# Pairing loads issued in halves, and a new slot table, in a four-block transformer kernel on one core

## The reference

```python
for i in range(DEPTH):
    x = attn_layer(shift_tokens(x), Wqkv[i], q_scale[i], k_scale[i], Wo[i]) + x
    x = ffn_layer(shift_tokens(x), ln_g[i], ln_b[i], W1[i], b1[i], W2[i], b2[i]) + x
# attn_layer: 16 heads of 64, q and k normalised and rotated; windows of 32 tokens
bk2, bv2 = (look(bk), look(bv))          # each window sees itself and the one before
attn = jax.nn.softmax(sim, -1)           # sim masked outside the band
out = jnp.einsum('bhwij,bhwje->bhwie', attn, bv2)
# ffn_layer: layer norm, x @ W1, a * gelu(gate), @ W2
```

## Time and profile before

| | us |
|---|---|
| median of 3 runs (lowest to highest) | 2043.94 (2038.4 to 2044.57) |
| the profiled execution | 2045.6 |
| its span | 2044.3 |
| PE busy, share | 1886.4, 92% |
| ACT, DVE, POOL busy | 1609.5, 1577.7, 1069.5 |
| granted TensorE clock, mean | 0.974 |

### The profile page before, as it was taken

How to read it: one execution, slowest core, us unless ns; L and a number is a source line. 1 busy time by engine, 2 the same in 40 slices (tenths; PEclk the granted TensorE clock), 3 DMA queues, 4 the chain that set the end, 5 groups by cost and what they waited for, 6 DMA issues and landing times.

```text
span 2044.3 us, 78892 instructions
## 1 busy us (share of the span) xinstructions
PE 1886.4 (92%) x34797; PEld 1592.2 (78%) x34797; DVE 1577.7 (77%) x2229; ACT 1609.5 (79%) x2835; POOL 1069.5 (52%) x523
## 2 busy tenths in 40 slices
PE   6999999678999999999999899999999998999986
PEld 4888888657887787877878777788788787887865
DVE  4556664677888798988889787988889788889873
ACT  2577777567898888888888888888788888888864
POOL 3100000366567575667566665758666576656520
PEclk9999999889999999999999999999999999999998
DMA  5000000033233334243332424344333334333421
GB/s 169 11 7 5 5 6 6 1 101 103 80 103 104 108 100 122 82 128 104 99 111 80 127 83 114 94 121 107 103 101 107 102 92 118 90 107 85 114 73 31
DMA packets 119822, 174.01 MB, mean 85 GB/s; under 512 B 25303, under 2 KB 44346, under 8 KB 119482
## 3 DMA queue, kind: packets, MB, share of 16 engines
q1 hardware_dynamic: 119308, 168.92, 29.8%
q10 hardware_dynamic: 174, 0.05, 0.0%
HBM read 117.54 MB, written 51.38 MB: 83 GB/s over the span
## 4 chain that ended last, share of the span: by engine, by line
PE 65%; ACT 13%; issue 8%; POOL 8%; DVE 6%; DMA 0%; POOLq 0%; ACTq 0%; SPq 0%; DVEq 0%
PE bank L705 7%; PE bank L855 6%; PE bank L682 6%; PE bank L684 5%; PE bank L683 5%; PE s_pair L727 5%; PE o_pair L756 4%; POOL rt L1703 3%; PE bank L609 3%; POOL rt L1694 3%; PE bank L768 3%; ACT t L1044 3%; PE bank L877 2%; ACT L1102 2%; PE bank L739 2%
## 5 line engine op out<-in xcount | busy, mean ns | idle before, releaser
L1694 POOL TENSOR_TENSOR rt<-raw,rot 128x1024 f32<-128x1024 f32 x192 | 456.5, 2378 | 343.6 <-PE bank L705 284.7
L1703 POOL TENSOR_TENSOR rt<-rt,t 128x2048 f32<-128x2048 f32 x96 | 439.8, 4582 | 142.5 <-DVE t L1497 138.5
L682 PE MATMUL bank<-wqkv_hi,xs 128*128 128x512 f32 x576 | 250.3, 435 | 24.7 <-ACT vn L1053 12.0
L1036 ACT ACTIVATE raw<-bank 128x512 f32<-128x512 f32 x384 | 230.0, 600 | 35.7 <-PE bank L684 15.1
L705 PE MATMUL bank<-const,rt 128*128 128x128 f32 x1536 | 221.7, 283 | 21.3 <-issue 9.8
L1505 DVE TENSOR_TENSOR rt<-rt,bank 128x2048 f32<-128x2048 f32 x96 | 219.6, 2288 | 18.2 <-POOL rt L1703 15.2
L684 PE MATMUL bank<-wqkv_hi,xs 128*128 128x512 f32 x576 | 230.9, 401 | 0.0
L683 PE MATMUL bank<-wqkv_lo,xs 128*128 128x512 f32 x576 | 230.3, 400 | 0.4 <-issue 0.4
L1497 DVE TENSOR_TENSOR t<-raw,bank 128x1024 f32<-128x1024 f32 x192 | 225.1, 1214 | 0.6
L1518 DVE TENSOR_REDUCE sm<-s_pair 128x16 f32<-128x1024 f32 x96 | 117.6, 1225 | 138.1 <-PE s_pair L727 137.7
L1484 DVE TENSOR_REDUCE bank<-t 128x32 f32<-128x2048 f32 x96 | 219.3, 2284 | 3.7 <-ACT t L1044 3.7
(11 more groups left out here) (413 smaller groups left out, 4489.1 us busy)
## 6 DMA issues: line engine op xcount, KB each, us to landing
v<-v_rows SPq DMA_DIRECT2D x288, 256.0 KB, 4.3
v_rows<-vn SPq DMA_DIRECT2D x192, 256.0 KB, 4.6
v<-v_rows SPq DMA_DIRECT2D x96, 192.0 KB, 3.1
wraw<-in_L_ffn_Wqkv_dram SPq DMA_DIRECT2D x36, 256.0 KB, 2.9
wo<-in_L_ffn_Wo_dram SPq DMA_DIRECT2D x6, 512.0 KB, 4.0
wraw<-in_L_ffn_W_in_dram SPq DMA_DIRECT2D x8, 256.0 KB, 2.7
w_out<-in_L_ffn_W_out_dram SPq DMA_DIRECT2D x8, 256.0 KB, 3.1
wraw<-in_L_ffn_W_dram SPq DMA_DIRECT2D x12, 170.5 KB, 2.3
```

The source lines that it names most:

```text
L682: pe.matmul(bank[:, :], hi, w[0][:, :], start=True, stop=False)
L1036: act.activation(k.raw_r[c][:, n * 512:(n + 1) * 512], k.one.at["qk", j][:, :], ACT.Copy)\
L1694: e = pool.tensor_tensor(heads(k.rt_r[c][:, part]), heads(k.raw_r[c][:, part]), cosv, ALU.mult)
L1703: pool.tensor_tensor(k.rt_r[c][:, :], k.rt_r[c][:, :], k.t2[:, :], ALU.add).then_inc(s["rot_add"], 1)
```

## The change

`pair_values(c)` becomes `pair_values(c, half)`, which issues two of the four loads; the waits stand in the first half. The two halves have slots of their own in `SP_AT`. All numbers of all tables are new. The core of the diff (of the tables, one pair of lines):

```diff
-ATTENTION_START, ATTENTION_SPACING = 7, 40
-EXPERTS_START, EXPERTS_SPACING = 71, 40
-LATE_START, LATE_SPACING = 391, 32
+ATTENTION_START, ATTENTION_SPACING = 6, 40
+EXPERTS_START, EXPERTS_SPACING = 70, 40
+LATE_START, LATE_SPACING = 372, 32
...
-SP_AT = dict(gain=9, w0=13, w1=13, w2=19, w3=19, st00=31, st01=43, st10=43, st11=43, w4=43, pair0=44, w5=63, pair1=73,
-             wo=114, w6=142, w7=148, w2d=181)
+SP_AT = dict(gain=26, w0=54, w1=72, w2=74, w3=76, st00=77, st01=79, st10=80, st11=86, w4=86, pair00=87, pair01=93,
+             w5=99, pair10=109, pair11=138, wo=169, w6=210, w7=210, w2d=221)
...
-        def pair_values(c):
+        def pair_values(c, half):
             v = 2 * u + c
-            sp.wait_ge(s[f"st_v{c}"], 32 * (u + 1))
-            if u:
-                sp.wait_ge(s["pe_o"], v - 1)
-            else:
-                sp.wait_ge(s["zero_kv"], ZEROS)
-            for half in range(2):
-                g0 = 1 if c == 0 and half == 0 else 0
...
+            if half == 0:
+                sp.wait_ge(s[f"st_v{c}"], 32 * (u + 1))
+                if u:
+                    sp.wait_ge(s["pe_o"], v - 1)
+                else:
+                    sp.wait_ge(s["zero_kv"], ZEROS)
+            g0 = 1 if c == 0 and half == 0 else 0
...
-        yield from t.to("pair0")
-        pair_values(0)
+        yield from t.to("pair00")
+        pair_values(0, 0)
+        yield from t.to("pair01")
+        pair_values(0, 1)
         yield from t.to("w5")
         next_chunk(5)
-        yield from t.to("pair1")
-        pair_values(1)
+        yield from t.to("pair10")
+        pair_values(1, 0)
+        yield from t.to("pair11")
+        pair_values(1, 1)
```

More of the change, by code:

```diff
@@ L158, in to @@
             yield
-ATTENTION_START, ATTENTION_SPACING = 7, 40
-EXPERTS_START, EXPERTS_SPACING = 71, 40
-LATE_START, LATE_SPACING = 391, 32
[L165 to L175, removed]
-             ln_sd_d=113, ln_out_d=113)
@@ new lines @@
+EXPERTS_START, EXPERTS_SPACING = 70, 40
+LATE_START, LATE_SPACING = 372, 32
+PE_A = dict(ln_sq_a=8, ln_sd_a=8, ln_out_a=12, features=19, k_features=32, q_features=32, sums=41, kv_turn=45,
+            quotient=45, norm0=52)
+PE_B = dict(ln_sq_b=8, ln_sd_b=8, ln_out_b=17, top2=17, weights=22, combine=27, expert0=34, expert1=36, expert2=44,
+            expert3=47, expert4=49, expert5=60, expert6=60, expert7=63, expert8=68, moe_out=74, ln_sq_c=75,
+            ln_sd_c=75, ln_out_c=79, scores=79, exp=79, threshold=96, spT=103, attend=107, back=114, ln_sq_d=118,
+            ln_sd_d=118, ln_out_d=118)
@@ new lines @@
+ACT_A = dict(ln_sq_a=6, ln_sd_a=6, ln_out_a=14, features=14, k_features=14, q_features=14, sums=40, kv_turn=42,
+             quotient=42, norm0=42)
+ACT_B = dict(ln_sq_b=0, ln_sd_b=0, ln_out_b=13, top2=13, weights=13, combine=25, expert0=29, expert1=32, expert2=36,
+             expert3=37, expert4=42, expert5=50, expert6=58, expert7=58, expert8=58, moe_out=68, ln_sq_c=71,
+             ln_sd_c=71, ln_out_c=74, scores=74, exp=74, threshold=86, spT=86, attend=86, back=106, ln_sq_d=113,
+             ln_sd_d=113, ln_out_d=113)
@@ new lines @@
+DVE_A = dict(ln_sq_a=0, ln_sd_a=13, ln_out_a=19, features=23, k_features=36, q_features=36, sums=36, kv_turn=51,
+             quotient=51, norm0=56)
+DVE_B = dict(ln_sq_b=0, ln_sd_b=14, ln_out_b=20, top2=23, weights=25, combine=34, expert0=36, expert1=42, expert2=50,
+             expert3=50, expert4=55, expert5=63, expert6=65, expert7=68, expert8=70, moe_out=76, ln_sq_c=76,
+             ln_sd_c=79, ln_out_c=80, scores=80, exp=89, threshold=89, spT=106, attend=109, back=115, ln_sq_d=115,
+             ln_sd_d=125, ln_out_d=125)
@@ new lines @@
+POOL_B = dict(ln_sq_b=0, ln_sd_b=0, ln_out_b=0)
+PE_AT = dict(qk00=35, qk01=36, qk02=36, qk03=37, qk10=46, qk11=50, qk12=54, qk13=54, v00=67, v01=68, v10=70, v11=70,
+             tqk00=72, tqk01=74, tqk02=81, tqk03=82, tqk10=83, tqk11=83, s00=83, tqk12=83, tqk13=83, s01=84, s10=93,
+             tp00=103, tp01=103, s11=105, a00=105, a01=113, tp10=120, tp11=124, to00=127, to01=130, a10=131, a11=131,
+             to10=137, to11=138, wo=147, mean=152, var=163, up0=176, up1=177, up2=177, down=188)
@@ new lines @@
+ACT_AT = dict(xs=8, qk00=24, qk01=26, qk02=27, qk03=27, sq0=32, qk10=39, norm0=42, qk11=42, qk12=46, qk13=49, sq1=51,
+              norm1=55, v00=55, v01=57, v10=60, v11=61, tqk00=62, tqk01=71, tqk02=73, tqk03=73, tqk10=77, tqk11=77,
+              tqk12=78, tqk13=78, exp0=87, tp00=94, tp01=94, exp1=106, tp10=115, tp11=118, to00=118, to01=119,
+              to10=127, to11=134, xf=141, lnsq=148, rstd=151, gelu0=168, gelu1=168, gelu2=168)
+DVE_AT = dict(ss0=41, sin0=48, nrm0=63, ss1=64, sin1=66, nrm1=77, smax0=90, ssum0=104, smax1=104, oa0=119, ssum1=119,
+              oa1=132, z_mid=145, xc=155, hn=161, hh0=171, hh1=171, hh2=172, z_out=192)
@@ L201 @@
+POOL_AT = dict(xs=43, zero=51, w0=75, cos0=80, w1=80, add0=92, w2=93, w3=93, cos1=94, add1=94, w4=99, w5=108, w6=192,
+               w7=235)
+SP_AT = dict(gain=26, w0=54, w1=72, w2=74, w3=76, st00=77, st01=79, st10=80, st11=86, w4=86, pair00=87, pair01=93,
+             w5=99, pair10=109, pair11=138, wo=169, w6=210, w7=210, w2d=221)
 SIGNALS = (
@@ L1824, in store_values @@
                 .then_inc(s[f"st_v{c}"], 16)
-        def pair_values(c):
+        def pair_values(c, half):
             v = 2 * u + c
-            sp.wait_ge(s[f"st_v{c}"], 32 * (u + 1))
-            if u:
-                sp.wait_ge(s["pe_o"], v - 1)
-            else:
-                sp.wait_ge(s["zero_kv"], ZEROS)
-            for half in range(2):
-                g0 = 1 if c == 0 and half == 0 else 0
[L1835 to L1839, removed]
+            if half == 0:
[5 more added lines that the diff above has]
+            g0 = 1 if c == 0 and half == 0 else 0
+            first = (NW * c + g0 - 1 + half) * WIN
+            for r in range(2):
+                at = 2 * WIN * r + WIN * half
+                src = k.v_rows[u % 2, first:first + (NW - g0) * WIN, r, :].rearrange("(g j) e -> j g e", j=WIN)
+                sp.dma_start(k.v2_r[c][at:at + WIN, g0:, :], src).then_inc(s[f"v2_{c}"], 16)
         t = Slots(SP_AT)
```

## The result

| | before | after |
|---|---|---|
| median of 4 runs each (lowest to highest), us | 2042.06 (2038.4 to 2044.57) | 2021.33 (2019.5 to 2024.43) |
| the profiled execution and its span, us | 2045.6, 2044.3 | 2024.43, 2023.1 |

After to before is 0.9901, with a 95% interval from 0.988 to 0.9923. The change gains 21 us. The forecast was 49 us (1995). Its sign held, and so did the wide range (1970 to 2030); the forecast's own range ended at 2020, just short, and the size did not hold.

A forecast was written before the change was run, and what follows sets the result against it. PE was taken as the bound, losing idle time to instruction holes behind value transfers and to the lower clock. 38 + 5 + 8 - 2 = 49 us off the profiled 2045.6, forecast 1995; own range 1970 to 2020, 8 in 10 1970 to 2030.

The forecast's parts named there:

- Item 1: SP's list: spreading the value transfers ends PE's instruction holes in attend of chunk 0; 38 us, plus 5 at the drain.
- the 43 with its drain: Gain from SP's new list: 38 us for the holes and 5 for the hole at 1966 us, where the last units drain.
- So it should not starve: Scores of chunk 0 begin after 1082.5, the second burst (1.5 MB) ends by 1080.7, so PE keeps its instructions.
- the clock's 15 us: Work lost over the six layers because the mean granted clock is 0.99; counted beside the 29.7 us of holes.
- Item 3: ACT's list: xs and one kT ahead of raw1, hidden by 0.3 us before PE's second transposes; 2 us lost, ends 0 and 23.
- Item 2: SP's moved half of v21 lands before attend of chunk 1 needs it, slack 8 us; cost 0.
- excess, five times: At layer changes SP's waits for POOL's weight splits may delay v21 loads, costing the lateness five times; taken as 0.
- Item 4: Start of the six layers: threshold work moved behind unit 0's normalisation and sum; gain 8 us, ends 0 and 12.0.
- Item 5: Block 0's tables, where PE's list changes too: a gain or loss up to 12.0 us, taken as 0.
- Rival 1: Holes move to the scores of chunk 0 behind the six-load burst, overlapping output weights' load; half stays, 2016 us; chance 0.13.
- Rival 2: Holes are not from the burst, or crossing an instruction block costs what it costs; 2038 us; chance 0.10.
- Rival 3: ACT's new order becomes the bound, raw1 late ahead of PE's second transposes every unit; slower, 2053 us; chance 0.07.

The follow-up runs named there:

- kernel 2: The changed kernel with SP's old list (v21's four loads together, v20's four together); 1.0025 of the kernel before.
- kernel 3: kernel 1 with POOL's sixth weight split (w5) one step earlier, ahead of the rotation of chunk 0; 0.9881 of the kernel before.
- kernel 4: The changed kernel with stores and pairing loads moving 16 of their 512 columns from unit 2 on; 0.9818 of the kernel before.
- kernel 5: The changed kernel with POOL's xs put back behind the rotation of chunk 0; 0.9838 of the kernel before.
- kernel 11: kernel 5 with the last two v21 loads held until PE ended the next unit's chunk 0 scores; 0.9762 of the kernel before, median 1989.7 us.
- kernel 1: The kernel before with only SP's list of the change, all other tables and the start old; 1.0004 of the kernel before.
- kernel 6: The changed kernel with the last sequence's sparse attention threshold ahead of unit 0's normalisation again; 0.9918 of the kernel before.

## Why the prediction was right in sign and wrong in size

*Item 1, the holes, is the step that failed*, in its sentence "The holes go". The mechanism stands: packets of instructions waited behind the values, and undoing the split brings the long holes back (kernel 2). The size does not. A hole has a part of its own, 1.15 us at this place with next to nothing in the queues, and the smaller burst leaves 1.70. I took the one unit in the earlier trace rows that passed the place as a sign that the place is free of holes unless a packet is late; that a packet must be due there I had written myself, and one that is due costs over a microsecond there with the queues empty too. Issue time fell by 12.3 us where I counted on 34.2 (29.7 and 4.5). Measured by itself item 1 is 22 to 27 us (kernels 2 and 3), against the 43 with its drain. The 43 are near what the transfers of the values cost in all: kernels 2 and 4 are 2.1% apart, 42 us, some 5 of them kernel 2's waits for weights. The split takes 22 to 25 of these and leaves 17 to 20. "So it should not starve", said of the second burst, failed with it: L727 lost 6.2 us, and splitting that burst took 16 us off kernel 5 (kernel 11).

*The terms that were not there.* The prediction priced SP's, ACT's and DVE's new lists and not POOL's, though POOL's is in the diff. Its `xs` ahead of the rotation cost 13 to 16 us in time (kernel 5): 10.7 at L768 and 9.8 of PE's busy time, in the profile. That is why only a part of the clock's 15 us came back: the long holes went and ten waits of 1.65 to 2.2 us came. The forecast had 28 us too much: item 1 accounts for 16 to 21 of them and this term for 13 to 16; item 3's 2 us, which were not lost, go the other way.

*Item 2, the moved half of `v21`, 0.* Right for this kernel, by a list that I had not priced. I named the waits for POOL's splits and the "excess, five times"; kernel 1 shows it at 14.8 us. The change avoids it because POOL's `w5` moved ahead of the rotation (kernel 3). The zero should have had that condition.

*Item 3, ACT's list, -2.* No wait of L705 for `raw` is in the profile. ACT's `raw` ends at 1067.97 us in an ordinary unit, and the block of transposes behind the output matrix begins at 1067.86 (1.04 us); its second half, which needs the bank, begins near 1068.4. So 0.4 us were to spare where the prediction had 0.3, and it cost 0. ACT's old list was not tried by itself.

*Item 4, the start, 8.* 6.2 us by kernel 6's profile, though its time does not settle it, and its cause as told: DVE serves unit 0 first, ACT waits 2.63 us for the square root's sum where it waited 8.03, PE 6.23 where it waited 9.7 (5 or less was forecast):

```profile
398.24 0.23 ACT L1110 ACTIVATE rn<-rn 128x32 f32<-128x32 f32 x1 [2.63 <-DVE rn L1486]
...
399.27 0.80 PE L682 MATMUL bank<-wqkv_hi,xs 128*128 128x512 f32 x1 [6.23 <-ACT vn L1053]
...
400.38 0.16 DVE L1414 RECIPROCAL e_small<-e_small 128x2 f32<-128x2 f32 x1
```

*Item 5, block 0, 0.* Not told from 0: kernel 3 with block 0's old lists has the first output matrix at 476.0 us, kernel 6 with the new ones and the old threshold at 475.2.

*The sum, as the runs have it:* 22 to 25 for the split, 6 for the start, 13 to 16 lost to POOL's `xs`: 12 to 18 of 21 us. The rest, 3 to 9 us, is within what the intervals of these ratios add up to, and no run assigns it.

*The rivals.* Rival 1 named the right place, L727 behind the burst of six, and 6.2 us of it came there; its price, 21 us, is near the 16 that kernel 11 won back. It did not need the output weights' load: 1.28 MB in six us was enough in an ordinary unit. Rival 2 is half right: crossing into a new block has a cost of its own, 8.6 of the 29.7 us. Rival 3 did not come. The slower rival should have been POOL's.

## What to carry to other kernels

When a list of every engine is renewed, price every engine's list, the one with the most idle time too: POOL idles over 40% of the span and its order cost more than the start brought. A DMA queue's list carries the waits of all that stands ahead of a load; a load that is moved later in it has to be read against each of them, at the rare places above all (here twice a layer). And where a hole has a cause that is shared by two parts, measure what is left with the cause at zero before counting on the whole, and ask whether the change brings the cause to zero or only makes it smaller.
